# A cross-attention kernel: GpSimd adds the probabilities ahead of the key norm's mean

## What is computed

```
q = (hidden @ Wq).reshape(B, Sq, H, D);  k = (context @ Wk).reshape(B, Skv, H, D);  v likewise
q = q * rsqrt(mean(q*q) + eps) * gq      # 16 heads, D = 128
k = k * rsqrt(mean(k*k) + eps) * gk      # the key norm: one number for each context row and head
attn = softmax(einsum('bqhd,bkhd->bhqk', q, k) / sqrt(D))
out = einsum('bhqk,bkhd->bqhd', attn, v).reshape(B, Sq, H*D) @ Wo
```

## Time and profile before

| | us |
|---|---|
| median of 3 runs | 1670.48 (1668.61 to 1671.59) |
| the profiled execution | 1675.99 |
| its span | 1674.2, mean granted clock 0.937 |
| GpSimd's first and last `key_mean` in the span | 149.2 and 1307.3 |

### The profile page before, as it was taken

How to read it: one execution, slowest core, us unless ns; L and a number is a source line. 1 busy time by engine, 2 the same in 40 slices (tenths; PEclk the granted TensorE clock), 3 DMA queues, 4 the chain that set the end, 5 groups by cost and what they waited for, 6 DMA issues and landing times. The chain is left out here.

```text
span 1674.2 us, 29041 instructions
## 1 busy us (share of the span) xinstructions
PE 1499.3 (90%) x6074; PEld 1001.1 (60%) x6074; DVE 1341.5 (80%) x2184; ACT 1137.0 (68%) x4750; POOL 940.8 (56%) x1469
## 2 busy tenths in 40 slices
PE   5997999999999999999999999999999697267776
PEld 3664666666666666666666666666666485134444
DVE  5787889888897988889898888989888556367785
ACT  5787778778777877877787787878787453223332
POOL 3004778777787877778787777878787400100000
PEclk9998999999999999999999999999999798667778
DMA  2100000000000000000000000000000200000000
GB/s 100 40 1 1 1 21 2 21 2 20 13 8 21 1 20 2 20 12 9 21 1 20 2 20 11 10 21 1 20 1 21 75 0 0 29 0 7 3 7 10
DMA packets 9815, 25.01 MB, mean 15 GB/s; under 512 B 736, under 2 KB 6144, under 8 KB 9520
## 3 DMA queue, kind: packets, MB, share of 16 engines
q1 hardware_dynamic: 9648, 23.49, 3.8%
HBM read 22.44 MB, written 1.05 MB: 14 GB/s over the span
## 5 line engine op out<-in xcount | busy, mean ns | idle before, releaser
L623 PE MATMUL psK<-wkh,c_cTh 128*124 128x512 f32 x832 | 511.3, 615 | 7.1 <-DVE c_prod L814 4.7
L814 DVE TENSOR_TENSOR c_prod<-psK,c_c 124x512 f32<-124x512 f32 x624 | 427.1, 685 | 69.8 <-PE psK L623 66.1
L973 POOL TENSOR_TENSOR c_acc<-c_acc,c_prob 123x1024 f32<-123x1024 f32 (+1 forms) x192 | 459.1, 2391 | 0.4 <-ACT c_prob L716 0.3
L643 PE MATMUL psO<-c_prob,raw 123*128 123x512 f32 (+1 forms) x832 | 427.0, 594 | 0.0
L831 DVE TENSOR_TENSOR c_prob<-psS,c_ss 124x512 f32<-124x512 f32 x416 | 286.9, 690 | 78.5 <-PE psS L634 60.7
L623 PE MATMUL psK<-wkl,c_cTh 128*124 128x512 f32 x832 | 330.0, 397 | 0.0
L710 ACT ACTIVATE c_unused<-c_prod 124x128 f32<-124x128 f32 x832 | 247.6, 299 | 119.6 <-DVE c_prod L814 119.6
L716 ACT ACTIVATE c_prob<-c_prob,shift 124x1024 f32<-124x1024 f32 x208 | 238.7, 1148 | 66.8 <-DVE c_prob L831 62.1
L821 DVE TENSOR_REDUCE c_ss<-c_prod 124x8 f32<-124x1024 f32 x208 | 253.8, 1220 | 7.2
L702 ACT ACTIVATE c_unused<-psK 124x128 f32<-124x128 f32 x832 | 218.8, 277 | 51.2 <-PE psK L623 36.9
L623 PEld LDWEIGHTS psK<-wkh,c_cTh 128*124 128x124 f32 x832 | 155.3, 187 | 145.1 <-issue 89.8
(11 more groups left out here) (301 smaller groups left out, 2420.7 us busy)
## 6 DMA issues: line engine op xcount, KB each, us to landing
raw<-in_ctx SPq DMA_DIRECT2D x16, 799.5 KB
raw<-in_L_xattn_Wq SPq DMA_DIRECT2D x3, 512.0 KB, 9.2
xs<-in_x SPq DMA_DIRECT2D x1, 1024.0 KB, 5.9
big<-in_L_xattn_Wk SPq DMA_DIRECT2D x1, 1024.0 KB, 8.5
qkv<-in_L_xattn_Wo SPq DMA_DIRECT2D x1, 1024.0 KB, 6.4
out<-s_y SPq DMA_DIRECT2D x8, 128.0 KB, 1.7
raw<-in_L_xattn_Wv SPq DMA_DIRECT2D x1, 832.0 KB, 4.3
o_wqkv<-in_L_attn_W_qkv SPq DMA_DIRECT2D x1, 768.0 KB, 9.3
```

Of the source, the lines that this page charges most:

```text
L623: last = nc.tensor.matmul(psK[0:ROWS, c % 2, :], x[:, slot, :], w[:, cols], start=(n == 0), stop=(n == len(terms) - 1))
L643: nc.tensor.matmul(psO[:, half, :], raw[0:rows, b, tile, :], prob[0:rows, probs(v), half * BANK:(half + 1) * BANK], start=(tile == 0), sto ...
L814: nc.vector.tensor_tensor(prod[:, k % 2, c - GRAM, :].rearrange("p (h c) -> p h c", c=CD), psK[0:ROWS, c % 2, :].rearrange("p (h c) -> p h ...
L973: nc.gpsimd.tensor_tensor(acc[0:rows, batch % 2, :], acc[0:rows, batch % 2, :], prob[0:rows, probs(s), :], ALU.add).then_inc(S.acc, 1)
```

## The change

GpSimd adds the exponentials first in its step, and `key_mean` then stands directly ahead of `key_root`. No instruction, no wait and no buffer is added or taken away.

```diff
                 e = s - 1 if s is not None and s > 0 else TP - 1 if s is None and v == TP - 2 else None
-                if r is not None:
-                    key_mean(i, r)
                 if e is not None:
                     add(i, e)
                 if r is not None:
+                    key_mean(i, r)
                     key_root(i, r)
```

## The result

| | before | after |
|---|---|---|
| median of 7 runs, us | 1672.12 (1668.61 to 1674.04) | 1679.81 (1676.19 to 1681.13) |
| ratio after / before | | 1.0046, 95% interval 1.0033 to 1.0059 |
| the profiled execution, us | 1675.99 | 1679.81 |
| its span, us | 1674.2 | 1678.1 |

The change makes the kernel 7.7 us slower, 0.46%. The engines' busy time, as the page of the kernel after has it, gives the first hint: VectorE is busy for 1385.2 us, where the kernel before had 1341.5, with the same instructions.

What follows compares the result with a forecast made beforehand. TensorE was taken to set the pace. Meetings cost 24.2 us and 11.8 comes back, net +12.4; with -1.5 for the clock, +11 us moves the median from 1670.48 to 1681.5 us, range 1667 to 1701.

Steps and rivals of the forecast that it cites:

- What bounds the kernel: Plain tiles: TensorE sets the pace, busy all 5.30 us; GpSimd matters only at TensorE's 14 waits for L902, 19.6 us.
- The collision: At n = 4 and 8 GpSimd's addition starts first and blocks VectorE's L878, 30 times; L878 ends 0.56 us after it.
- The price at n = 8: L831 starts 1.77 us late; TensorE loses 1.11 us in 9 batches (10.0) and 1.79 in 6 with a back edge (10.7).
- The price at n = 4: L831 starts 1.24 us late; TensorE loses 0.23 us at chunk 0 in 15 batches, 3.5 us.
- What comes back: TensorE's shorter wait for L902: 7 x 0.3 = 2.1 us, 6 x 1.5 = 9.0 with a back edge, 0.7 in batch 0.
- The clock: Three granted-clock drops behind the longest waits: up to 5.3 us saved, new idle pieces could cost 1.75 each; -1.5 us taken.
- Rival 1: At L878: no or negligible blocking when GpSimd is first; some 14 us gained, perhaps 5 more of clock, 1654 us; chance 0.12.
- Rival 3: Full price: no slack regained, 30 meetings cost 1.77 us each, 53 us less 12 given back, 1712 us; chance 0.12.
- Rival 2: A wash: VectorE's slack covers most of the meetings, or GpSimd doesn't get ahead of L878; 1668 to 1673 us; chance 0.10.

Runs made afterwards that it cites:

- the last pair: Query parts earlier, measured again: on the kernel before, 1644.45 us, ratio 0.9827; on the changed kernel with newton_end ahead of key_sums, 1643.24 us, 0.983.
- The run with 8 columns: Changed kernel with newton_end (L878) on 8 of its 512 columns at the same place: 1665.15 us, ratio 0.9969 to the kernel before.
- the run without meetings: Changed kernel with VectorE running newton_end ahead of key_sums at n = 3 and 7 instead of behind it: 1654.78 us, ratio 0.9911 to the kernel before.

## Why the prediction was right

The forecast was +11 us, from 1670.5 to 1681.5; measured were +7.7 (1672.12 to 1679.81). The mechanism held. Two numbers came out nearer than their working deserved, by luck, as said below. By its steps:

- **What bounds the kernel** held: TensorE sets the pace, and GpSimd matters at L902 alone. The run with the query parts earlier shows the full worth of that wait, and the last pair shows that nothing measurable is left beyond it.
- **The collision** held in every part. It was foreseen for 30 of 30 meetings with L831 1.77 us late at n = 8; 30 came, and L831 came 2.37 instead of 0.60 behind the start of L878, that is 1.77 late. The 0.56 us between the end of GpSimd's operation and that of VectorE's, taken from L473 in the query stage, was 0.55 here. The run with 8 columns confirms that the whole addition is waited for. As to the Trainium skill (SBUF — State Buffer, Who interferes with whom), the runs agree with its rule on the side that matters here, GpSimd first, and with its remark that the order of issue decides who blocks.
- **The price at n = 8** was 20.7 us in the sum (10.0 and 10.7) and measures 19.1. From one of TensorE's transposes to the next it is 1.15 a batch without a back edge (6.45 us instead of 5.30; 1.11 expected). That the two agree so well is in part luck: I had let TensorE wait at chunk 0 for the product of chunk 2, 1.55 us behind L831. The trace has the wait one chunk earlier, at chunk 3 for the product of chunk 1, and behind it chunk 0 finds its product ready (574.04 + 0.67 = 574.71, chunk 0 at 575.00), since VectorE without its pauses needs only 1.39 us from L831 to that product. With a back edge I had taken the whole 1.77, put down as 1.79, but it is 1.4 (1.15 and 0.24 in the tile at the back edge). VectorE regains part of its lag before its pause: from L831 to L821 it takes 3.30 us (645.68 to 648.98) instead of 3.56 (645.51 to 649.07), and the pause itself is 2.02 instead of 2.09. The line of the kernel before, and those of the kernel after:

```profile
645.51 0.68 DVE L831 TENSOR_TENSOR c_prob<-psS,c_ss 124x512 f32<-124x512 f32 x1
```

```profile
645.68 0.68 DVE L831 TENSOR_TENSOR c_prob<-psS,c_ss 124x512 f32<-124x512 f32 x1
...
648.98 1.22 DVE L821 TENSOR_REDUCE c_ss<-c_prod 124x8 f32<-124x1024 f32 x1
...
652.22 0.69 DVE L831 TENSOR_TENSOR c_prob<-psS,c_ss 124x512 f32<-124x512 f32 x1 [2.02 <-PE psO L643]
```

- **The price at n = 4** was too small: 3.5 us expected, 6.0 measured, 0.40 a batch instead of 0.23. I had read the lead at chunk 0 alone. TensorE is already late at chunk 3, which starts 0.05 us after the product of chunk 1 ends (551.41 and 551.46), and loses a little again in the next tile (0.12).
- **What comes back** was 11.8 us of wait and 1.5 of clock. The wait gave 19.6 - 7.9 = 11.7, but only as a sum: the 7 waits without a back edge shrank by 4.0 us instead of 2.1 and the 6 with one by 7.1 instead of 9.0, so that the agreement is luck. The clock was the term under-sized: all three drops went away, 4.8 us in the profiled executions, while the new waits, none over 1.0 us, brought none. Of the terms this is the largest miss, and in the profiles the reason why the forecast is 3 us too high; for the medians that stays open, since other executions with such waits have one or two drops.
- **Rival 1** (no blocking, 1654) fell with L878 at 2.44 us, but its sum was right: the run without meetings measured 1654.78. **Rival 3** (full price) fell, since a meeting that costs VectorE 1.77 us costs TensorE 0.40 or 1.15. **Rival 2** (a wash) fell, as the interval of the change (1.0033 to 1.0059) lies above its 1668 to 1673 us.

## What to carry to other kernels

Before moving work on GpSimd, look at what VectorE does in the stretch that it moves into. In every meeting seen here an instruction of VectorE with two inputs in SBUF and a GpSimd operation that reads SBUF took turns, and the one that came second paid for the rest of the first (1.76 us for VectorE behind an addition, 0.24 for GpSimd's mean behind L878); the profile books that as a long instruction and not as a wait, so compare maximum and median duration of a line. Where they must overlap, let the long one come second (the addition then took 2.80 us instead of 2.39) or cut it in two, and ask first whether the wait that the move should shorten can be removed by an earlier start of its producer: here one table was worth 1.7%, the reordering at best 0.9%, and both together no more than the table.

## What the runs showed of the hardware that I had not expected

- An idle stretch of TensorE costs more than its length, by an amount that doesn't grow with it: at a full granted clock tiles with waits for L902 of 0.54, 1.10 and 1.77 us take 6.12, 6.69 and 7.35 us between transposes instead of 5.30, that is 0.28 to 0.29 more than the wait each time. So shortening a wait gives back its length, and only removing it gives back the rest.
- The blocked instruction gives the next one trouble too. GpSimd's mean behind the addition takes 0.53 us instead of 0.20, since L878 goes first once the addition ends; with an L878 of 8 columns it stays at 0.20.
